# First transform of four spectral layers on four 64x64 tiles of TensorE

## What is computed

```python
xs = jnp.fft.rfft2(xf32, axes=(1, 2))            # 64 rows, 33 columns of frequencies
xs = xs.reshape(B, H, Wm, NUM_HEADS, BLOCK)      # 8 blocks of 48 channels
o1r = relu(xr @ w1[0] - xi @ w1[1] + b1[0])      # per block, complex 48x48, o1i alike
o2r = o1r @ w2[0] - o1i @ w2[1] + b2[0]          # o2i alike
out = softshrink(o2)                             # by 0.01, real and imaginary
return irfft2(out) + bias                        # bias is the layer's input
```

## Time and profile before

| | |
|---|---|
| median of 3 runs | 2126.09 us (2120.29 to 2128.18) |
| the profiled execution | 2126.64 us, of which its span is 2124.7 us |
| mean granted TensorE clock | 0.984 of full speed |
| PE (TensorE matmul) busy | 2012.0 us, 95% of the span, 32256 records |
| PEld (TensorE weight load) busy | 1706.3 us, 80% |
| DVE (VectorE) busy | 1151.1 us, 54% |
| ACT (ScalarE) busy | 875.4 us, 41% |
| POOL (GpSimd) busy | 439.2 us, 21% |

### The profile page before, as it was taken

How to read it: one execution, slowest core, us unless ns; L and a number is a source line. 1 busy time by engine, 2 the same in 40 slices (tenths; PEclk the granted TensorE clock), 3 DMA queues, 4 the chain that set the end, 5 groups by cost and what they waited for, 6 DMA issues and landing times.

```text
span 2124.7 us, 70981 instructions
## 1 busy us (share of the span) xinstructions
PE 2012.0 (95%) x32256; PEld 1706.3 (80%) x32256; DVE 1151.1 (54%) x2462; ACT 875.4 (41%) x1470; POOL 439.2 (21%) x425
## 2 busy tenths in 40 slices
PE   5999995899998999999999999999899999999996
PEld 4787772787875999999999999999788878887874
DVE  2686887865644433333333333332366666666674
ACT  2544445444433333333333333333355444444542
POOL 3212013965531000100011000000321211220300
PEclk9999997999999999999999999999999999999999
DMA  9425738307326111111111111114703564457314
GB/s 157 100 48 81 125 59 138 56 5 125 80 74 159 31 30 31 30 30 30 30 30 30 30 30 30 30 30 71 126 16 61 87 107 85 81 89 125 60 33 93
DMA packets 299706, 141.20 MB, mean 66 GB/s; under 512 B 275632, under 2 KB 298032, under 8 KB 299440
## 3 DMA queue, kind: packets, MB, share of 16 engines
q1 hardware_dynamic: 299440, 137.11, 35.3%
HBM read 74.17 MB, written 62.91 MB: 65 GB/s over the span
## 4 chain that ended last, share of the span: by engine, by line
PE 84%; DVE 10%; issue 2%; DMA 1%; SPq 1%; POOL 0%; ACT 0%; DVEq 0%; ACTq 0%; POOLq 0%
PE ps L595 19%; PE ps L580 19%; PE ps L444 8%; PE ps L458 8%; PE ps L502 8%; PE ps L428 7%; PE ps L517 6%; PE ps L475 6%; DVE u L791 4%; PE ps L483 2%; DVE st L830 2%; DVE clamp L785 1%; DVE xs L818 1%; PE ps L565 1%; DMA xs<-in_x 1%
## 5 line engine op out<-in xcount | busy, mean ns | idle before, releaser
L933 DVE TENSOR_TENSOR gl<-g,gh 128x512 fp32r<-128x512 f32 x192 | 156.7, 816 | 476.5 <-ACT gh L736 476.5
L791 DVE TENSOR_TENSOR u<-ps,clamp 64x192 f32<-64x192 f32 (+1 forms) x864 | 378.0, 437 | 27.7
L444 PEld LDWEIGHTS ps<-const,z 128*48 128x48 f32 x8384 | 279.6, 124 | 109.0 <-issue 99.8
L733 ACT ACTIVATE g<-ps,colp 128x512 f32<-128x512 f32 x192 | 132.6, 690 | 529.1 <-PE ps L580 529.1
L444 PE MATMUL ps<-const,z 128*48 128x64 f32 (+1 forms) x8384 | 278.8, 217 | 7.5 <-issue 5.4
L677 ACT ACTIVATE h<-ps,w 113x512 f32<-113x512 f32 (+2 forms) x280 | 171.2, 611 | 257.1 <-PE ps L458 257.1
L595 PE MATMUL ps<-w2h,gh 128*128 128x384 f32 x768 | 261.8, 341 | 0.0
L785 DVE TENSOR_SCALAR clamp<-ps 128x384 f32<-128x384 f32 (+1 forms) x216 | 112.9, 522 | 271.7 <-PE ps L475 271.7
L428 PE MATMUL ps<-const,xn 128*64 128x64 f32 x6144 | 224.0, 228 | 38.0 <-POOL xn L1020 21.2
L595 PE MATMUL ps<-w2h,gl 128*128 128x384 f32 x768 | 258.5, 337 | 0.0
L595 PE MATMUL ps<-w2l,gh 128*128 128x384 f32 x768 | 257.5, 335 | 0.0
(11 more groups left out here) (69 smaller groups left out, 2477.1 us busy)
## 6 DMA issues: line engine op xcount, KB each, us to landing
after<-xs SPq DMA_DIRECT2D x96, 384.0 KB, 5.4
xs<-after SPq DMA_DIRECT2D x94, 384.0 KB, 8.6
after<-om SPq DMA_DIRECT2D x32, 384.0 KB, 4.4
out<-xs SPq DMA_DIRECT2D x32, 384.0 KB, 5.4
xm<-after SPq DMA_DIRECT2D x30, 384.0 KB, 6.2
xs<-in_x SPq DMA_DIRECT2D x24, 384.0 KB, 9.0
wstage<-in_spectral SPq DMA_DIRECT2D x16, 210.0 KB, 7.1
xs<-in_x SPq DMA_DIRECT2D x4, 768.0 KB, 11.8
```

The lines of the kernel that those rows point to most:

```text
L444: mm = pe.matmul(ps[a * SIDE:a * SIDE + BLOCK, F2_BANK, n * L.kh:(n + 1) * L.kh], z[:, g % 2, slot, :], basis(col + a * SIDE, L.kh), start ...
L791: dve.tensor_tensor(u[to, g % 2, :, start + b:start + size:BATCH], whole, limited, ALU.subtract).then_inc(u_ready, 1)
L933: dve.tensor_tensor(gl[:, n % 4, :], g[:, n % 2, :], gh[:, n % 4, :], ALU.subtract).then_inc(g_low, 1)
```

## The change

A call of f1 now covers 16 channels (two chunks, a `TWIN`), three calls for each block. The stationary operand is one channel of one image, 64 rows by 64 columns, and the moving operand is the 64 x 64 transform (real and imaginary in its 64 columns), which lies twice in the constants, once for each image. So each matmul uses a 64x64 tile: rows by image `b`, columns by the channel's parity `j`. The image also picks the bank, so a call fills both banks. In PSUM, partitions are (parity, h) and columns (channel pair, real or imaginary, frequency), while `z` has partitions (real or imaginary, h); ScalarE makes that exchange in four copies of 64 partitions, two in the slot of the call and two in the next. The slots are `[1, 4, 7]` (full) and `[1, 4, 6]` (layer 2). A call waits until all four copies of the one before are done. The slots of `centre` stay as they were (`centre_at`), and the waits of GpSimd count double calls.

```diff
+TWINS = CHUNKS // 2
+PIECES = ((0, 0), (0, 1), (1, 1), (1, 0))
+SPREAD = len(PIECES)
...
-        self.f1_at = [0, 1, 3, 5, 7, 8] if self.full else [0, 1, 3, 4, 6, 7]
+        self.f1_at = [1, 4, 7] if self.full else [1, 4, 6]
+        self.centre_at = [0, 1, 3, 4, 6, 7]
...
-                n = CHUNKS * g + k
+                n = TWINS * g + k
+                chunk = 2 * n + 1
...
-                    pe.wait_ge(xt_ready, n + 1 - (CHUNKS * BLOCKS if L.index > 1 else 0))
-                if n >= 2:
-                    pe.wait_ge(z_ready, n - 1)
+                    pe.wait_ge(xt_ready, chunk + 1 - (CHUNKS * BLOCKS if L.index > 1 else 0))
+                if n >= 1:
+                    pe.wait_ge(z_ready, SPREAD * n)
                 for c in range(CHAN):
-                    for a in range(2):
-                        mm = pe.matmul(ps[a * SIDE:(a + 1) * SIDE, F1_BANKS[n % 2], c * SPAN:(c + 1) * SPAN],
-                                       xn[:, n % RING, c, :], basis(C_D1 + a * SPAN, SPAN), start=True, stop=True)
+                    slot, first = (chunk - 1 + c // (CHAN // 2)) % RING, c % (CHAN // 2) * 2
+                    for b in range(BATCH):
+                        rows = slice(b * SIDE, (b + 1) * SIDE)
+                        for j in range(2):
+                            mm = pe.matmul(ps[j * SIDE:(j + 1) * SIDE, F1_BANKS[b], c * SPAN:(c + 1) * SPAN],
+                                           xn[rows, slot, first + j, :], const[rows, C_D1:C_D1 + SPAN],
+                                           start=True, stop=True)
                 mm.then_inc(f1_done, 1)
...
-            def f1(g, k):
-
-                n = CHUNKS * g + k
-                act.wait_ge(f1_done, n + 1)
-                act.activation(z[:, g % 2, :, k * CHAN:(k + 1) * CHAN],
-                               ps[:, F1_BANKS[n % 2], :].rearrange("p (c s) -> p s c", s=SPAN),
-                               ACT.Copy, scale=layer_of(g).forward).then_inc(z_ready, 1)
+            def f1(g, k, pieces):
+
+                act.wait_ge(f1_done, TWINS * g + k + 1)
+                for j, a in pieces:
+                    mine, to = slice(j * SIDE, (j + 1) * SIDE), slice(a * SIDE, (a + 1) * SIDE)
+                    first = 2 * k * CHAN + j
+                    act.activation(z[to, g % 2, :, first:first + 2 * CHAN - 1:2].rearrange("p (k b) c -> p k b c", b=BATCH),
+                                   ps[mine, F1_BANKS[0]:F1_BANKS[1] + 1, :]
+                                   .rearrange("p b (c a k) -> p a k b c", a=2, k=HALF)[:, a],
+                                   ACT.Copy, scale=layer_of(g).forward).then_inc(z_ready, 1)
...
                         if t in L.f1_at and g + 1 < last:
-                            f1(g + 1, L.f1_at.index(t))
+                            f1(g + 1, L.f1_at.index(t), PIECES[0:2])
+                        if t - 1 in L.f1_at and g + 1 < last:
+                            f1(g + 1, L.f1_at.index(t - 1), PIECES[2:4])
...
-                    pool.wait_ge(f1_done, n - RING + 1)
+                    pool.wait_ge(f1_done, (n - RING) // 2 + 1)
...
-    d1 = np.einsum("wak,bd->bwakd", col, np.eye(BATCH)).reshape(P, 2 * SPAN)
+    d1 = np.tile(col.reshape(SIDE, SPAN), (BATCH, 1))
```

More of the change, by code:

```diff
@@ L42 @@
 SIGNS = 5
-C_D1, C_D2, C_D2A, C_D2B, C_SIGN = [P * n for n in range(5)]
+C_D1 = 0
+C_D2, C_D2A, C_D2B, C_SIGN = [SPAN + P * n for n in range(4)]
 C_ID, C_D5, C_D5H, C_D6, C_COLS = [C_SIGN + SIGNS + P * n for n in range(5)]
@@ L420, in f1 @@
                 elif L.norm:
-                    pe.wait_ge(xn_ready, n - CHUNKS * (BLOCKS + 1) + 1)
+                    pe.wait_ge(xn_ready, chunk - CHUNKS * (BLOCKS + 1) + 1)
                 else:
-                    pe.wait_ge(xt_ready, n + 1 - (CHUNKS * BLOCKS if L.index > 1 else 0))
-                if n >= 2:
-                    pe.wait_ge(z_ready, n - 1)
+                    pe.wait_ge(xt_ready, chunk + 1 - (CHUNKS * BLOCKS if L.index > 1 else 0))
+                if n >= 1:
+                    pe.wait_ge(z_ready, SPREAD * n)
                 for c in range(CHAN):
-                    for a in range(2):
-                        mm = pe.matmul(ps[a * SIDE:(a + 1) * SIDE, F1_BANKS[n % 2], c * SPAN:(c + 1) * SPAN],
-                                       xn[:, n % RING, c, :], basis(C_D1 + a * SPAN, SPAN), start=True, stop=True)
+                    slot, first = (chunk - 1 + c // (CHAN // 2)) % RING, c % (CHAN // 2) * 2
[5 more added lines that the diff above has]
+                                           start=True, stop=True)
                 mm.then_inc(f1_done, 1)
@@ L435, in f2 @@
                 if t == 0:
-                    pe.wait_ge(z_ready, CHUNKS * (g + 1))
+                    pe.wait_ge(z_ready, SPREAD * TWINS * (g + 1))
                     if g == 0:
@@ L522, in spectral @@
             def spectral(first, last):
-                for k in range(CHUNKS):
+                for k in range(TWINS):
                     f1(first, k)
@@ L626, in _ @@
         def _(act):
[L628 to L634 removed]
+            def f1(g, k, pieces):
[7 more added lines that the diff above has]
+                                   ACT.Copy, scale=layer_of(g).forward).then_inc(z_ready, 1)
             def normalise_row(r):
                 if r == 0:
[L639 removed]
+                    act.wait_ge(f1_done, TWINS * BLOCKS)
                     act.wait_ge(x_loaded[buffer_of(PAIRS)], LOADS * (uses_before(PAIRS) + 1))
@@ L697, in spectral @@
                         normalise_row(r)
-                for k in range(CHUNKS):
-                    f1(first, k)
+                for k in range(TWINS):
+                    f1(first, k, PIECES)
                 for g in range(first, last):
@@ L878, in spectral @@
                             m2(g - 1, layer_of(g - 1).n - 1)
-                        if norm and t in L.f1_at:
-                            n = CHUNKS * (g + 1 - first) + L.f1_at.index(t) + AHEAD
+                        if norm and t in L.centre_at:
+                            n = CHUNKS * (g + 1 - first) + L.centre_at.index(t) + AHEAD
                             if n < CHUNKS * (last - first):
@@ L1025, in keep @@
                 data, channel = channels(g, k), n * CHAN
-                pool.wait_ge(f1_done, CHUNKS * BLOCKS + n + 1)
+                pool.wait_ge(f1_done, TWINS * BLOCKS + n // 2 + 1)
                 scale = lnrow[:, 0, channel:channel + CHAN].unsqueeze(2).to_broadcast([P, CHAN, SIDE])
```

## The result

The changed kernel takes 2155.07 us (median of 4 runs, 2148.34 to 2158.94) where the kernel before, measured beside it, takes 2124.65: a ratio of 1.0141, 95% interval 1.0108 to 1.0173. It is slower by 30 us, where I had forecast 23 less. The profiled execution took 2154.99 us, its span is 2153.2 and the mean granted clock of TensorE 0.973 of full speed (0.984 before). In this kernel f1 is line 437, f2 454, m1 468, m2 485 or 493, f5 512, f6 527; ScalarE's copies to `z` are line 644, DVE's subtraction 806, and on GpSimd the weights begin at line 1007 and `turn` is line 1035.

The account below looks back on a forecast made before the run. PE was taken as the bound, with 84% of the chain. Layers 3 and 4 (-7.7), layer 1 (-2.1) and layer 2 (-14.2) sum to -24.0 us from 2126.64, giving 2103 us (chance 0.50), range 2092 to 2187.

Parts of the forecast that it names:

- The pace: f1 on PE: four matmuls run in the time of two, so a double call takes 0.93 us instead of 1.87.
- rival (a): f1 on PE: row halves run in turn, a double call costs 0.94 us more, 2183 us in all; chance 0.24.
- (b): f1 on PE: a 21.3 ns floor between matmul starts, 0.43 us more per double call, 2138 us; chance 0.16.
- the break-even of 18.9 ns: f1 on PE: any pace slower than 18.9 ns per matmul, 0.28 us more per double call, loses.
- Slot 0: Start of a full-layer block: with f1's cover for zf lost, the next m1 begins 2.8 us in, not 2.47.
- DVE's loop: Slot 8 of a full-layer block: clamp and four subtractions hold m2, so it gets no shorter than 3.54 us.
- a plain block of layer 2: Layer 2, blocks after the first two: 2.35 us less each than 34.31, after giving back 0.55 for centring.
- ScalarE's pieces: Four copies to z per double call, 0.60 us each (bounds 0.50 and 0.80), hidden inside a block.
- the sum: Slot times added to a full-layer block of 35.6 us against 36.48; over all stages, -24.0 us.
- the one sentence on GpSimd: GpSimd's transposes ahead of f1: six chunks of cover, priced at nothing; without it 1.1 us per pair.
- a little clock loss: Start of layers 3 and 4: part of 11.5 us for PE and ScalarE taking turns, 3.7 us more than before.
- (c): Pieces of 0.8 us at two exposed starts, or missed stalls in slots 0, 7, 8: 11 us, 2114; chance 0.10.

## Why the prediction was wrong, by its own steps

**Right.** The pace: a double call on four tiles costs what one old call did, 14.7 ns a record, so neither rival (a) nor (b) came, and the break-even of 18.9 ns was kept. One reading behind it was off: line 565 is a transpose that leaves one record each, and four in a row take 0.60 us with 0.27 for the last, so 0.86 ns per column and not 1.2. The half-width records are 1.9 times as fast and not over twice, which still fits two column halves at work. The Trainium skill ("TensorE: Matmul & The Clock Gate", Wait — 56ns, not 53.3ns?) has a start-to-start floor of about 25 ns; the mean of 14.7 ns does not agree with it when four tiles take turns, while the 26.7 ns with the rows in turn lie above it. Slot 0 at 2.80 (2.8 said) and slot 8 at 3.49 (3.54 said, DVE's loop) were right, and so was a plain block of layer 2: block 10 took 31.93 us by f2's records, and 34.31 - 2.35 = 31.96 was the forecast. ScalarE's pieces are hidden inside a block: of f2's waits for `z`, 8.6 us in four, all but 0.5 us are the three starts (2.7 each).

**Nearly right.** Slots 1, 4 and 7 are 3.96, 5.25 and 4.38 us where the sum had 3.85, 5.16 and 4.28. So a double call costs 1.26 us there and not 1.16, which makes the block 35.86 and not 35.6. The boundary ahead is 1799.53 - 1798.53 = 1.00 for f2 against 0.89 (0.11, I said 0.10), f1 to f5 is 1.09 for 0.93 (0.16, I said 0.13), and the f5 behind it is 0.05 longer, which I had not counted. The parts that I named for DVE's loop (0.56 + 4 x 0.49 + 0.9 us) make 3.4 us and not the 3.68 of the rows; the forecast went by the rows. ScalarE's pieces take 640 ns, not 600, within the bounds.

**The step that failed** is the one sentence on GpSimd: "POOL's turning waits for whole double calls but holds six chunks and works on the next block, so I price it at nothing; without that cover it would be 1.1 us for each pair". It looks at the transposes alone. In GpSimd's queue stands, between chunk 2 and chunk 3 of every second block, a wait of up to 40 us for a DMA, and the cover was some 0.8 us for one call. The change moves the need for chunk 3 one slot ahead. The price is five waits, 18.9 us together, and with the half clock behind most of them 22.5 us in all. The row was in the trace of before and said `POOL L992 ... [40.45 <-DMA wstage<-in_spectral]`; I passed over it as idle time of an engine that is not the bottleneck.

**Mis-sized terms.** The difference of the spans is +28.5 us where the sum said -24, by stage:

| | said | measured |
|---|---|---|
| layer 1, start and first two blocks | +0.4 | +2.3 |
| layer 1, blocks 2 to 6 | -2.6 | +6.2 |
| layer 2 with its start | -14.2 | -5.5 |
| layers 3 and 4, start | +3.7 | +5.8 |
| layers 3 and 4, blocks 16 and 17 | -0.3 | +2.3 |
| the eight plain full blocks (18, 19, 21, 23, 25, 27, 29, 30) | -6.8 | -4.7 |
| blocks 20, 22, 24, 26 and 28 | -4.2 | +22.0 |

Of the 52.5 us between the two columns, 22.5 are GpSimd's wait (shown by taking it away in two ways). The starts and the blocks next to them are 6.6 us over by the table, and the extra banks gave back 9.6 us in all: I had the pieces and their 2.4 us, but took "a little clock loss" for what is half clock in all three double calls, 1.99 us each, and let the first two blocks of layer 1 absorb the rest. The pauses without a releaser are 30.7 us in the waits view, against 19.4 before, 11 more; that most of them come with the loads is shown. That there are more of them after the change is seen in every trace with whole loads (24 to 31 us against 16 to 19), though with short loads the two kernels gained nearly the same (16 and 13 us). Block 6 of layer 1 is a case: 38.5 to 41.6 us in the changed kernel's eight traces with alternating rows, 36.8 to 37.2 in the old f1's four without a long wait for GpSimd there. The prediction had no term for pauses at all. The steady block is 0.24 us longer than said, some 4 us in all. Some 8 us stay open (the parts overlap, so the split is an estimate), most of it in layer 2, where blocks 11 and 13 gave nothing.

**The form of the result.** None of my rivals held this. (c) had "stalls in slots 0, 7 and 8 that I missed" at 11 us; the stall was in slot 4, and at twice the size. The range reached it only because (a) and (b) needed the room. The list of what would show it wrong had PE waiting for `z`, and not for `xn`.

## What to carry to other kernels

When a step begins to take two buffers at once, it asks for the second one sooner: go to the engine that fills it and read everything in its queue between the two, with what each of them waits for, before the cover is called enough. Idle time of 40 us on an engine that is not the bottleneck is a warning if what stands behind it is needed within a microsecond of its end. A small load that an engine waits for goes ahead of bulk loads in the queue (26 us here), and a pair of buffers that becomes one unit needs a second pair wherever nothing else runs beside it.

## What the runs showed of the hardware

- Four 64x64 tiles ran at 14.7 ns a record, but only with the row halves alternating in the order of issue; with all of one image first it was 26.7 ns with the same instructions. The Trainium skill ("TensorEngine Tiling (Array Packing)", Key Properties) says that tiles load weights and multiply independently of each other; the trace agrees for neighbours in the order of issue, and the run with the rows in turn shows that the order decides.
- A change of tile shape costs 0.11 us on the way in, and 0.16 and 0.05 on the way out.
- Turn-taking between PE and ScalarE costs twice: the granted clock was 0.54 in a window where PE was busy for 10.94 of 22 us, and the same matmuls took 1.99 us and not 1.16. Each wait of 4.5 to 10 us for GpSimd was followed by groups at the lower level too (1.90, 1.98 and 1.92 us for what takes 1.16, 1.14 and 1.15).
- PE stopped for 1 to 4 us inside groups that were ready while row loads were in flight. With a quarter of the bytes the pauses of blocks 22 to 29 were gone, and the two kernels were 13 and 16 us faster. What it is in the loads that stops PE stays open.
